# Busy TensorE products ahead of four norms and routings, and the last expert combine moved to TensorE, in a macaron block

## The chip, the cores and the metric

One core of one Trainium2 chip. The metric is the device time of one execution in microseconds (us); the time of a kernel is the median of its runs. Engines in the profile: PE is TensorE (PEld its weight loads), DVE is VectorE, ACT is ScalarE, POOL is GpSimd, SP is SyncE; SPq and POOLq are the queues from which SP and POOL start transfers. The clock granted to TensorE is printed as a share: 1.00 is 2.4 GHz, 0.50 is 1.2 GHz.

## The reference, cut to what matters

Four sequences of 256 tokens with 256 channels, all fp32. LN is a layer norm without gains.

```python
x += 0.5 * moe(LN(x))           # 64 experts, top 6 of a softmax, 64 slots each, plus a shared SiLU expert
x += attn16(LN(x))              # 16 heads, rotary, causal
x += 0.5 * moe(LN(x))           # the same weights again
x += 0.5 * wave(LN(x))
x += gqa(LN(x))                 # 16 query heads, 4 key heads
x += 0.5 * wave(LN(x))

def wave(x):
    h = (cos(ph) + sin(ph)) * sigmoid(x @ amp_w + amp_b)      # ph = pi * tanh(x @ ph_w + ph_b)
    for l in range(2):
        h = LN(h + (h @ ent_w[l] + ent_b[l]) @ ent_pw[l] + ent_pb[l])
        h = LN(h + sum over two paths of (h @ path_w[l, q] + path_b[l, q]) * mod[l, q])
    return h
```

In `moe` every token's row goes to the slots of its six experts, and its result is the sum of six expert rows, each times its weight. This sum of six rows is the *combine*.

## The kernel before, in words

The 1024 tokens are 8 tiles of 128, two for a sequence, and `m.x` holds them in SBUF for the whole program. PSUM is eight banks (`m.banks`). The program is a row of blocks; inside a block every engine has its own list of instructions in written order, and semaphores join the lists. Between two blocks all engines meet at a barrier.

**first_phase** routes the four sequences, one turn each. `norm_tensor` (L172) turns the normed tokens, `route_tensor` (L282) makes the router's logits (L238), half of the shared expert (L246), the rank of each token among those that chose the same expert (L255 to L258, it waits for DVE's choice mask), the other half, and the shared expert's output. DVE makes the slots (L383), and POOL sends the rows out with 12 indirect transfers (L434).

**experts_phase** runs the 64 experts over what SP loads from the slots (L700). **middle_phase** gathers and combines the first MoE, runs attention by sequence and routes again; three of the four routings run beside the attention of the next sequence, and the last stands alone after it, with `norm_tensor` and `route_tensor` in a row. `ahead(0, step)` is the first sequence's norm and projections (L172, L922). **experts_phase** then runs again.

`keep_busy(n)` (L931) issues n bf16 products of 128x384 into PSUM that nobody reads. The kernel before has it inside attention only.

**fold_phase** does two things at once. It folds the wave weights: `ent_w @ ent_pw` on PE (L1733, L1738), the path weights times `mod` on DVE, then bias, mean and last-row corrections. Beside that it combines the second MoE: POOL gathers 48 pieces of 128 rows (L1610), and DVE adds each to x with one multiply-add (L1634, and L1645 for the last sequence). Sequences share two buffers, so POOL waits for `s_combined`. When tiles 0 to 3 are done, POOL takes the root of their variance (L1968, L1970), DVE applies the norm (L1915), and PE and ACT begin the wave's first products (`wave_tensor_x`: turn L1801, product L1814; ACT takes tanh and a sine argument).

**last_phase** does the same for tiles 4 to 7, and meanwhile finishes the folded maps (`finish_maps`, L1539 to L1561, with `split_bias` L1521 to L1527 and `bias_for_last_row` L1534) and the attention weights (L1564 to L1571); POOL adds a bias to x over all tiles (L1985). Then ACT takes eight sines, DVE forms u (L1928), and 32 items (4 steps by 8 tiles) go through PE, ACT, DVE and a POOL root for each (L1968, L1970). Attention and the second wave follow.

## Time and profile before

| what | us |
|---|---|
| median of three runs (784.13, 786.36, 787.07) | 786.36 |
| profiled execution | 787.34 |
| span in its trace | 785.7 |
| PE busy | 577.7 (74%) |
| DVE busy | 389.2 (50%) |
| POOL busy | 295.2 (38%) |
| ACT busy | 233.4 (30%) |

The profiled execution lies 0.98 us above the median, and 1.6 us of it lie outside the span. Times inside the trace count from the start of the span. Busy times are sums over all stages; in one stage an engine can wait for the whole time while another sets the pace.

### The profile page before, as it was taken

To read this page: it belongs to the slowest core of one execution; us is meant where nothing else is said; L and a number is where in the kernel's file an instruction comes from. 1 tells how busy PE (TensorE), PEld (TensorE's weight loads), DVE (VectorE), ACT (ScalarE), POOL (GpSimd) and SP (SyncE) were. 2 spreads that over 40 slices of the span, in tenths; PEclk is the share of its full clock that TensorE was granted. 3 is DMA by queue.
4 is the path that set the end of the run, shared out by engine and by line. 5 is a ranking of instruction groups with operands and counts; after the bars stand their busy time and mean duration, and the time that the engine had idled before them with its cause. 6 is when DMAs were issued, how large, how long until landed. Compare 5 with 4: busy or idle time off the path is not lost. (4 is left out here: it accounts for less than half of the span.)

```text
span 785.7 us, 10359 instructions
## 1 busy us (share of the span) xinstructions
PE 577.7 (74%) x3486; PEld 368.9 (47%) x3486; DVE 389.2 (50%) x1102; ACT 233.4 (30%) x638; POOL 295.2 (38%) x383
## 2 busy tenths in 40 slices
PE   2666259970799999998953398984336697897796
PEld 1334125530466666665632254564213586554485
DVE  4656213333475676855442033366758547624135
ACT  1222024440132232321310144420033463142664
POOL 0556611106601537160326012257754266003065
PEclk9757569995799999998985599987577798998899
DMA  8886048842200314340166168733370000000001
GB/s 322 290 295 215 16 129 271 282 164 80 73 9 1 81 41 85 35 170 4 37 241 138 55 211 301 243 104 98 89 80 1 0 1 1 1 1 0 2 1 53
DMA packets 39723, 82.96 MB, mean 106 GB/s; under 512 B 7805, under 2 KB 27906, under 8 KB 38816
## 3 DMA queue, kind: packets, MB, share of 16 engines
q1 hardware_dynamic: 26144, 45.03, 17.7%
q0 software_dynamic: 13248, 37.07, 17.2%
q8 instruction: 25, 0.41, 0.2%
q10 hardware_dynamic: 288, 0.30, 0.1%
q14 instruction: 18, 0.15, 0.1%
HBM read 60.21 MB, written 26.35 MB: 110 GB/s over the span
## 5 line engine op out<-in xcount | busy, mean ns | idle before, releaser
L434 POOL DMA_INDIRECT expert_in<-xn_sent,scatter_slots x72 | 70.9, 985 | 79.7 <-DVE slots L383 50.5
L770 DVE SCALAR_TENSOR_TENSOR work<-work,banks 128x96 f32<-128x96 f32 x64 | 16.3, 254 | 124.1 <-ACT work L750 124.1
L1845 PE MATMUL banks<-w_gu,w_dn 128*128 128x256 f32 x256 | 68.4, 394 | 0.0
L1610 POOL DMA_INDIRECT w_dn<-expert_out,slots x48 | 51.3, 1069 | 26.4 <-issue 14.2
L790 PE MATMUL banks<-ident,work 128*128 128x128 f32 x128 | 29.5, 316 | 42.6 <-DMA work<-expert_in 42.6
L1251 POOL DMA_INDIRECT w_gu<-expert_out,gather_slots x48 | 49.3, 1028 | 28.7 <-DVE gather_slots L1259 14.7
L799 PE MATMUL banks<-w_gu,work 128*64 128x192 f32 x512 | 58.5, 352 | 0.0
L1968 POOL TENSOR_TENSOR var_eps<-mv,eps 128x1 f32<-128x1 f32 (+1 forms) x70 | 13.7, 195 | 116.8 <-ACT w_dn L1894 55.2
L1845 PEld LDWEIGHTS banks<-w_gu,w_dn 128*128 128x128 f32 x256 | 46.0, 199 | 4.2
L790 PEld LDWEIGHTS banks<-ident,work 128*128 128x128 f32 x128 | 13.8, 149 | 67.5 <-issue 41.5
L1970 POOL TENSOR_TENSOR rstd<-var_eps,minus_half 128x1 f32<-128x1 f32 (+1 forms) x70 | 42.4, 606 | 5.5
L1933 DVE TENSOR_SCALAR w_dn<-banks,rstd 128x255 f32<-128x255 f32 x48 | 23.2, 483 | 37.2 <-POOL rstd L1970 37.2
L812 PE MATMUL banks<-w_dn,work 96*64 96x256 f32 x256 | 41.4, 404 | 0.0
L746 ACT COPY work<-banks 128x256 f32<-128x256 f32 x64 | 23.8, 372 | 54.0 <-PE banks L790 54.0
L799 PEld LDWEIGHTS banks<-w_gu,work 128*64 128x64 f32 x512 | 32.6, 142 | 14.3 <-issue 11.2
L172 PE MATMUL banks<-ident,xn 128*128 128x128 f32 x24 | 5.3, 358 | 43.9 <-DVE xn L151 27.0
L1192 DVE TENSOR_REDUCE w_dn<-banks 128x2 f32<-128x256 f32 x64 | 31.6, 549 | 9.1 <-PE banks L978 8.7
L756 ACT COPY work<-banks 128x256 f32<-128x256 f32 x64 | 23.8, 372 | 36.0 <-PE banks L812 35.9
L1835 PE MATMUL banks<-ident,w_dn 128*128 128x128 f32 x128 | 25.7, 292 | 11.9 <-DVE w_dn L1928 11.9
L246 PE MATMUL banks<-w_sgu,work 128*128 128x384 f32 x64 | 34.1, 681 | 0.0
L1128 ACT ACTIVATE w_dn<-banks 128x768 f32<-128x768 f32 x32 | 26.0, 811 | 26.9 <-PE banks L1007 26.6
L163 POOL TENSOR_TENSOR rstd<-var_eps,minus_half 128x2 f32<-128x2 f32 x8 | 5.7, 713 | 74.9 <-DVE var_eps L142 48.8
(271 smaller groups left out, 1258.0 us busy)
## 6 DMA issues: line engine op xcount, KB each, us to landing
work<-expert_in SPq DMA_DIRECT2D x64, 128.0 KB, 3.8
expert_out<-work SPq DMA_DIRECT2D x64, 128.0 KB, 3.8
w_gu<-in_gate_up SPq DMA_DIRECT2D x10, 768.0 KB
w_gu<-in_gate_up POOLq DMA_DIRECT2D x6, 768.0 KB, 5.6
expert_in<-w_dn SPq DMA_DIRECT2D x4, 1024.0 KB, 7.5
w_dn<-in_down SPq DMA_DIRECT2D x10, 384.0 KB
w_gu<-in_gate_up SPq DMA_DIRECT2D x1, 3840.0 KB, 12.0
w_dn<-in_down SPq DMA_DIRECT2D x1, 3072.0 KB, 25.8
```

The lines of the kernel that those rows point to most:

```text
L246: last = nc.tensor.matmul(r.p_shared[t][:, 0:2 * SHID], r.xnT[:, c, t * P:(t + 1) * P], m.w_sgu[:, c, :], start=(c == 0), stop=(c == KC - 1))
L434: nc.gpsimd.indirect_dma_start(out=m.expert_in, out_offset=bass.IndirectOffsetOnAxis(m.scatter_slots[u][:, at:at + 1], 0), in_=xn[:, t, :] ...
L790: last = nc.tensor.transpose(p_rowsT[b % 2][:, c, :], rows[b][:, c * P:(c + 1) * P], m.ident[:, :])
L799: last = nc.tensor.matmul(p_gu[b % 2][half], rowsT[b % 2][:, c, half], w_gu[:, pair * 2 + e, c, :], start=(c == 0), stop=(c == KC - 1))
L812: last = nc.tensor.matmul(p_out[b % 2][half], hiddenT[b % 2][0:HID, half], w_dn[:, pair * 2 + e, :], start=True, stop=True)
L1128: nc.scalar.activation(a.pT[p % SLOTS3], a.p_pairs[p % SLOTS3], ACT.Exp).then_inc(s.probs, 1)
L1192: last = nc.vector.tensor_reduce(a.qk[:, tile, head + at:head + at + 2, DH], a.p_pairs[(p + 1) % SLOTS3][:, :, cols], AX.X, ALU.max, negat ...
L1251: nc.gpsimd.indirect_dma_start(out=rows[:, at, :], out_offset=None, in_=m.expert_out, in_offset=bass.IndirectOffsetOnAxis(m.gather_slots[: ...
L1610: nc.gpsimd.indirect_dma_start(out=w.combined[q % 2][:, t * TOPK + k, :], out_offset=None, in_=m.expert_out, in_offset=bass.IndirectOffset ...
L1835: last = nc.tensor.transpose(f.p_turn[t % DEEP][:, c, :], u[:, t, c * P:(c + 1) * P], m.ident[:, :])
L1845: last = nc.tensor.matmul(f.p_lin[t % DEEP], f.uT[t % DEEP][:, c, :], w.lin[:, step, c, :], start=(step > 0 and c == 0), stop=(c == KC - 1))
L1970: nc.gpsimd.tensor_tensor(m.rstd[:, group], m.var_eps[:, group], m.minus_half[:, group], ALU.pow).then_inc(done, 1)
```

## The change

Three edits.

1. `keep_busy` takes a bank. `route_tensor` issues 4 unread products ahead of the logits, 14 ahead of the rank and 4 ahead of the shared output, in the four turns of the first phase and in the last routing. In the middle phase PE waits until the first sequence's expert rows have been gathered and then issues 16 ahead of the first norm, and 14 ahead of the last routing's norm.
2. The fold moves into the last phase: one block less. `finish_maps` becomes `scale_maps` and `finish_qkv`, called from the fold's DVE list.
3. The second combine moves to PE. ACT writes each weight column as a 128x128 diagonal (a ring of 8), PE multiplies it with the gathered rows, six products a tile added up in PSUM (`sum_tile`), and DVE adds the sum to x (`add_sum`). The rows have seven homes, and the last tile takes the first home again, so POOL's last six gathers wait for tile 0's sum. The norm goes by tiles 0 to 3, 4 and 5, 6 and 7. All eight sines come behind the last product.

```diff
 def route_tensor(nc, m, r, eng, s, ready, turn, then=None):
+    keep_busy(nc, m, 4, FREE_BANK)
     route_tensor_logits(nc, m, r, eng, s, ready)
     route_tensor_shared(nc, m, r, s, 0)
+    keep_busy(nc, m, 14, FREE_BANK)
     route_tensor_rank(nc, m, r, eng, s, turn)
...
+    keep_busy(nc, m, 4, FREE_BANK)
     route_tensor_out(nc, m, r, eng, s, turn)
...
-def keep_busy(nc, m, n):
+def keep_busy(nc, m, n, bank=2):
...
+            pe.wait_ge(comb.gathered[TB - 1], 16 * TOPK)
+            keep_busy(nc, m, 16)
             for step in range(3):
                 ahead(0, step)
...
+            keep_busy(nc, m, 14)
             norm_tensor(nc, m, pe, norm, 2 * B - 1, m.xn_sent, p_norm)
             route_tensor(nc, m, r, pe, sr, (norm.xnT, 2 * B), 2 * B - 1)
...
+def fold_pool(nc, m, w, s, wave, pool):
+    for t in range(TILES):
+        if t == 7:
+            pool.wait_ge(s.summed, 1)
+        for k in range(TOPK):
+            nc.gpsimd.indirect_dma_start(
...
+        if t == 5:
+            norm_roots_pool(nc, m, wave, pool, 0, [0])
+        if t == 6:
+            norm_roots_pool(nc, m, wave, pool, 0, [1])
+    norm_roots_pool(nc, m, wave, pool, 0, [2])
...
+def fold_vector(nc, m, w, f, s, wave, dve, chain):
...
+    for k in range(1, STEPS):
+        nc.vector.tensor_copy(w.shift_wide[:, k - 1], w.shift_cols[:, k - 1, :].unsqueeze(2).broadcast_to([P, KC, P])
+                              ).then_inc(s.wide, 1)
+    add_sum(0)
+    add_sum(1)
...
+    scale_maps(nc, w, dve, chain, s.scaled)
+    for t in range(2, 4):
+        add_sum(t)
+    stats_all_vector(nc, m, wave, chain, range(0, 4))
+    add_sum(4)
+    split_bias(nc, m, w, chain)
+    apply_all_vector(nc, m, f, wave, dve, 0, range(0, 4))
+    for k in range(1, STEPS):
+        dve.wait_ge(s.last_steps, k)
+        bias_for_last_row(nc, m, chain, w.lin[:, k], m.banks[:, 4 + k, 0:D], w.bias[:, 2 + k, :])
+    dve.sem_inc(s.maps, 1)
+    add_sum(5)
+    stats_all_vector(nc, m, wave, chain, range(4, 6))
+    dve.wait_ge(s.small, 4 * 16)
+    finish_qkv(nc, w, chain)
+    add_sum(6)
+    stats_all_vector(nc, m, wave, chain, range(6, 7))
+    apply_all_vector(nc, m, f, wave, dve, 0, range(4, 6))
+    add_sum(7)
+    stats_all_vector(nc, m, wave, chain, range(7, 8))
+    apply_all_vector(nc, m, f, wave, dve, 0, range(6, 8))
...
+    sum_tile(0)
+    sum_tile(1)
+    for k in range(1, STEPS):
+        step_shift(k)
+    sum_tile(2)
+    sum_tile(3)
+    pe.wait_ge(s.scaled, 1)
...
+    sum_tile(4)
+    pe.wait_ge(s.maps, 1)
+    wave_tensor_x(nc, m, w, f, wave, pe, 0, range(0, 4), f.p_turn_x)
+    sum_tile(5)
+    sum_tile(6)
+    wave_tensor_x(nc, m, w, f, wave, pe, 0, range(4, 6), f.p_turn_x)
+    sum_tile(7)
+    wave_tensor_x(nc, m, w, f, wave, pe, 0, range(6, 8), f.p_turn_x)
```

TensorE in one routing turn of the first phase, before: the logits, half of the shared expert, the rank and the other half.

```order
L238 MATMUL banks<-w_router,work 128x64 [waits norm_normed_T_ready]
L238 MATMUL banks<-w_router,work 128x64 x3
L246 MATMUL banks<-w_sgu,work 128x384 x2
L255 MATMUL banks<-work,before_b 128x64 [waits route_choice_mask_ready]
L256 MATMUL banks<-taken,ones_b 128x64
```

The same place in the changed kernel, whose line numbers are its own; L937 is `keep_busy`.

```order
L937 MATMUL banks<-causal_b,ident_b 128x384 x4
L241 MATMUL banks<-w_router,work 128x64 [waits norm_normed_T_ready]
L241 MATMUL banks<-w_router,work 128x64 x3
L249 MATMUL banks<-w_sgu,work 128x384 x2
L937 MATMUL banks<-causal_b,ident_b 128x384 x14
L258 MATMUL banks<-work,before_b 128x64 [waits route_choice_mask_ready]
```

The busy products stand ahead of each wait, so the logits and the rank are queued behind them.

GpSimd in the fold, before: gathers, the first norm's root, the last gathers, the barrier and the second root.

```order
L1610 DMA w_dn<-expert_out,slots 128x256 x24
L1610 DMA w_dn<-expert_out,slots 128x256 [waits sequence_combined]
L1610 DMA w_dn<-expert_out,slots 128x256 x11
L1968 TENSOR_TENSOR var_eps<-mv,eps 128x4 [waits wave_x_variance_ready,sequence_combined]
L1970 TENSOR_TENSOR rstd<-var_eps,minus_half 128x4 [waits wave_eps_added]
L1610 DMA w_dn<-expert_out,slots 128x256 x12
```

GpSimd at the same place in the changed kernel: L1613 is a gather, L2034 and L2036 are a norm's root.

```order
L1613 DMA w_dn<-expert_out,slots 128x256 x24
L1613 DMA work<-expert_out,slots 128x256 x12
L2034 TENSOR_TENSOR var_eps<-mv,eps 128x4 [waits wave_x_variance_ready]
L2036 TENSOR_TENSOR rstd<-var_eps,minus_half 128x4 [waits wave_eps_added]
L1613 DMA w_qkv<-expert_out,slots 128x256 x6
L2034 TENSOR_TENSOR var_eps<-mv,eps 128x2 [waits wave_x_variance_ready]
L2036 TENSOR_TENSOR rstd<-var_eps,minus_half 128x2 [waits wave_eps_added]
L1613 DMA w_dn<-expert_out,slots 128x256 [waits tile_summed]
L1613 DMA w_dn<-expert_out,slots 128x256 x5
```

The last six gathers (tile 7) now stand behind the root of tiles 4 and 5, which waits for DVE's statistics of these tiles.

TensorE in the changed kernel, from the sum of tile 4 (L1763) to the sum of tile 6; L1866 turns, L1879 multiplies.

```order
L1763 MATMUL banks<-work,w_dn 128x256 [waits weight_diagonal_ready,last_rows_gathered_tile4,tile_sum_added]
L1763 MATMUL banks<-work,w_dn 128x256 [waits weight_diagonal_ready] x5
L1866 MATMUL banks<-ident,w_dn 128x128 [waits wave_x_normed,step_maps_ready]
...
L1879 MATMUL banks<-w_gu,w_dn 128x512 [waits wave_x_T_ready]
L1879 MATMUL banks<-w_gu,w_dn 128x512
L1763 MATMUL banks<-work,w_dn 128x256 [waits weight_diagonal_ready,last_rows_gathered_tile5,tile_sum_added]
L1763 MATMUL banks<-work,w_dn 128x256 [waits weight_diagonal_ready] x5
L1763 MATMUL banks<-w_qkv,w_dn 128x256 [waits weight_diagonal_ready,last_rows_gathered_tile6,tile_sum_added]
```

The first wave products of tiles 0 to 3 now wait for the finished maps (`step_maps_ready`), and the sums of tiles 5 to 7 come behind them.

## Rows read from the trace of the kernel before

**Rows 1.** The page's part 4: the chain that ended last, by engine.

```profile
issue 9%; POOL 6%; PE 5%; DVE 3%; POOLq 0%; ACT 0%; DVEq 0%
```

**Rows 2.** Timeline, PE, first routing turn: start, length, line, operation, idle before and releaser.

```profile
16.01 1.97 PE L238 MATMUL banks<-w_router,work 128*128 128x64 f32 x8 [0.67 <-ACT work L179]
...
22.16 0.20 PE L255 MATMUL banks<-work,before_b 128*128 128x64 bf16 x1 [1.84 <-DVE work L349]
```

**Rows 3.** Timeline, second turn: DVE's slots, and POOL's first scatter.

```profile
42.52 0.17 DVE L383 COPY slots<-scatter_slots 128x12 uint32<-128x12 uint32 x1
...
48.83 0.97 POOL L434 DMA_INDIRECT expert_in<-xn_sent,scatter_slots  x1 [6.91 <-remote]
```

**Rows 4.** Timeline, PE, a stretch of the second attention at the full clock.

```profile
242.18 2.82 PE L922 MATMUL banks<-w_qkv,w_gu 128*128 128x512 f32 x8
...
252.00 3.41 PE L931 MATMUL banks<-causal_b,ident_b 128*128 128x384 bf16 x20
...
256.53 1.10 PE L238 MATMUL banks<-w_router,work 128*128 128x64 f32 x8 [0.68 <-ACT work L179]
```

**Rows 5.** Timeline, DVE and PE, ahead of the first attention.

```profile
194.03 3.09 DVE L1275 SCALAR_TENSOR_TENSOR x<-w_gu,cur_weights,x 128x256 f32<-128x256 f32 x6 [4.87 <-DMA w_gu<-expert_out,gather_slots]
...
199.88 1.08 PE L172 MATMUL banks<-ident,xn 128*128 128x128 f32 x4 [27.04 <-DVE xn L151]
201.63 8.37 PE L922 MATMUL banks<-w_qkv,w_gu 128*128 128x512 f32 x16 [0.67 <-ACT w_gu L179]
```

**Rows 6.** Timeline, PE and SP's queue, the last routing and the load behind it.

```profile
404.75 0.76 PE L172 MATMUL banks<-ident,xn_sent 128*128 128x128 f32 x4 [3.56 <-DVE xn_sent L151]
406.18 1.97 PE L238 MATMUL banks<-w_router,work 128*128 128x64 f32 x8 [0.68 <-ACT work L179]
...
441.61 8.53 SPq L700 DMA_DIRECT2D work<-expert_in  x8
```

**Rows 7.** Timeline, PE, fold and first wave.

```profile
515.86 9.99 PE L1733 MATMUL banks<-w_gu 128*128 128x256 f32 x32 [2.69 <-PEq L694]
...
594.66 1.54 PE L1801 MATMUL banks<-ident,w_dn 128*128 128x128 f32 x6 [17.70 <-DVE w_dn L1915]
596.00 3.62 PE L1814 MATMUL banks<-w_gu,w_dn 128*128 128x512 f32 x4
...
599.84 5.46 PE L1814 MATMUL banks<-w_gu,w_dn 128*128 128x512 f32 x12
```

**Rows 8.** Timeline, POOL, DVE and ACT, fold and first wave.

```profile
566.61 1.04 POOL L1970 TENSOR_TENSOR rstd<-var_eps,minus_half 128x4 f32<-128x4 f32 x1
...
582.48 1.00 POOL L1610 DMA_INDIRECT w_dn<-expert_out,slots  x1 [0.30 <-issue]
...
588.68 3.09 DVE L1645 SCALAR_TENSOR_TENSOR x<-w_dn,weights,x 128x256 f32<-128x256 f32 x6 [5.67 <-DMA w_dn<-expert_out,slots]
...
606.75 1.28 ACT L1885 ACT_TABLE_LOAD   x1
...
615.20 2.77 DVE L1928 SCALAR_TENSOR_TENSOR w_dn<-w_dn 128x256 f32<-128x256 f32 x8
```

**Rows 9.** Four stretches: length; PE, PEld, DVE, ACT, POOL busy; clock, DMA share, GB/s.

```profile
524.73:532.27 7.54, 7.54 (x37) 6.65 (x36) 7.06 (x14) 0.00 (x0) 6.02 (x6) 1.00 0.35 102
563.26:565.30 2.04, 2.04 (x6) 1.59 (x6) 1.97 (x2) 0.00 (x0) 1.43 (x3) 0.50 0.39 96
595.49:598.93 3.44, 3.44 (x8) 1.73 (x7) 3.41 (x4) 1.02 (x3) 3.28 (x1) 0.50 0.00 0
602.46:612.84 10.38, 4.40 (x13) 2.01 (x11) 9.81 (x25) 7.41 (x16) 0.13 (x1) 0.88 0.01 2
```

**Rows 10.** DVE's groups by line in the fold: busy, mean ns, idle before.

```profile
L1545 DVE TENSOR_SCALAR w_gu<-w_gu 128x4 f32<-128x4 f32 x1 | 3.5, 3476 | 0.0
...
L1903 DVE BATCH_NORM_STATS2 stats<-x 128x6 f32<-128x256 f32 x8 | 3.0, 418 | 0.4
...
L1717 DVE TENSOR_TENSOR w_gu<-w_gu,banks 128x256 f32<-128x256 f32 x3 | 1.3, 420 | 1.2 <-PE banks L1746 1.1
```

More of the change, by code:

```diff
@@ L1477, in last_weights @@
     w.parts = [g[:, first:first + 128].bitcast(BF16) for first in (8192, 8960, 3072)]
-    w.combined = [flat(d, 10240 + 3072 * b, (TB * TOPK, D)) for b in range(2)]
+    one = TOPK * D
+    homes = [d[:, 10240 + one * b:10240 + one * (b + 1)] for b in range(4)]
+    homes += [m.work[:, 0:one], m.work[:, one:2 * one], m.w_qkv[:, :, :].rearrange("p c n -> p (c n)"), homes[0]]
+    w.combined = [home.rearrange("p (k d) -> p k d", d=D) for home in homes]
     return w
@@ L1556, in finish_maps, with finish_qkv @@
     eng.sem_inc(s_scaled, 1)
-    split_bias(nc, m, w, chain)
-    for k in range(1, STEPS):
-        eng.wait_ge(s_last, k)
-        bias_for_last_row(nc, m, chain, w.lin[:, k], m.banks[:, 4 + k, 0:D], w.bias[:, 2 + k, :])
-    eng.sem_inc(s_ready, 1)
+def finish_qkv(nc, w, chain):
     for c in range(KC):
@@ new lines, with __init__ @@
+class Fold:
+    def __init__(self, sem):
+        self.small = sem("small_last_weights_loaded")
+        self.prod, self.read = sem("fold_product_ready"), sem("fold_products_read")
+        self.wide = sem("bias_columns_spread")
+        self.halved, self.last = sem("amplitude_map_halved"), sem("last_row_of_input_maps_ready")
+        self.sin, self.half = sem("phase_sines_ready"), sem("phase_reduced")
+        self.gathered = [sem(f"last_rows_gathered_tile{t}") for t in range(TILES)]
+        self.diag, self.used = sem("weight_diagonal_ready"), sem("weight_diagonal_used")
+        self.summed, self.added = sem("tile_summed"), sem("tile_sum_added")
+        self.maps, self.scaled, self.last_steps = sem("step_maps_ready"), sem("step_maps_scaled"), sem("last_row_of_step_maps_ready")
@@ new lines, in fold_scalar, with diagonals @@
+def fold_scalar(nc, m, w, f, s, wave, act):
+    def diagonals(t):
+        for k in range(TOPK):
+            j = t * TOPK + k
+            if j >= DIAGS:
+                last_used = j - DIAGS
+                if last_used % TOPK == TOPK - 1:
+                    act.wait_ge(s.summed, last_used // TOPK + 1)
+                else:
+                    act.wait_ge(s.used, last_used - last_used // TOPK + 1)
+            nc.scalar.activation(w.diag[j % DIAGS], m.ident[:, :], ACT.Copy, scale=m.weights[:, t, k:k + 1]
+                                 ).then_inc(s.diag, 1)
+    act.wait_ge(s.half, 1)
+    nc.scalar.activation(w.phase_sin, w.phase_turns, ACT.Sin).then_inc(s.sin, 1)
+    act.wait_ge(s.half, 2)
+    nc.scalar.activation(w.phase_cos, w.phase_cos, ACT.Sin, scale=-1.0, bias=w.half_pi).then_inc(s.sin, 1)
+    for t in range(6):
+        diagonals(t)
+    wave_scalar_x(nc, w, f, wave, act, 0, range(0, 4))
+    diagonals(6)
+    diagonals(7)
+    wave_scalar_x(nc, w, f, wave, act, 0, range(4, 6))
+    wave_scalar_x(nc, w, f, wave, act, 0, range(6, 8))
@@ L2027, in _ @@
         def _(dve):
[L2028 removed]
             chain = Chain(dve, v_chain)
[L2030 to L2031 removed]
+            fold_vector(nc, m, w, f, fold, wave, dve, chain)
+            wave_vector(nc, m, w, f, wave, dve, chain, 0)
             dve.wait_ge(s_pad, 3)
@@ L2044, in _ @@
         def _(pe):
-            def last_rows():
-                pe.wait_ge(s_scaled, 1)
-                pe.wait_ge(wave.tanh, TILES)
-                for k in range(1, STEPS):
-                    nc.tensor.matmul(m.banks[:, 4 + k, 0:D], w.last_row, w.lin[:, k, KC - 1, :], start=True, stop=True
-                                     ).then_inc(s_last, 1)
-            wave_tensor(nc, m, w, f, wave, pe, 0, s_maps, REST, last_rows)
+            fold_tensor(nc, m, w, f, fold, wave, pe)
+            wave_tensor(nc, m, w, f, wave, pe, 0, fold.maps)
             for t in range(TILES):
```

360 lines of the change are left out of this document (164 added, 196 removed).

## The prediction

> **What bounds the kernel now.** I read the chain that ended last first. No engine holds it: the largest share is issue, and POOL, PE and DVE have a few per cent each [rows 1]. So time is won or lost in the waits of single stages, and I went through the timelines of the four stages that the change touches.
>
> In the first routing, PE waits 0.67 us for the turned norm and 1.84 us for DVE's choice mask [rows 2]. From the second turn on the route is not what POOL waits for: DVE has the slots at 42.7, and POOL's first scatter starts at 48.83, released by the completion of the turn before it [rows 3]. Six microseconds of slack lie between them. Only a delay of the first turn reaches the end.
>
> Ahead of the first attention PE has been idle for 27.04 us, and then it works at the lower clock: the 16 projection passes take 8.37 us [rows 5], where 8 of the same take 2.82 us in a stretch at the full clock [rows 4]. Ahead of the last routing PE is idle for 3.56 us, and its logits take 1.97 us [rows 6] against 1.10 us at the full clock [rows 4].
>
> The fold is the long case. The first wave can't go on before DVE forms u at 615.20 [rows 8]. Three chains end near there: POOL's gathers (the last is issued at 582.48, and DVE has its rows at 588.68, 5.2 us after the issue ended); PE's cold products of tiles 4 to 7, from 594.66 to 605.3 [rows 7]; and DVE's finish of the maps, which ends last. DVE's list runs without a hole into u; the sines that ACT makes behind its table load of 1.28 us are there before. So the change has to beat u's start at 615.20.
>
> **The change part by part.**
>
> *First routing.* A busy product is 3.41 / 20 = 0.17 us at the full clock [rows 4]; the logits double at the lower one, so I take 0.30 to 0.34 us there. The 4 ahead of the logits need up to 1.3 us where the hole is 0.67: the logits start some 0.6 us late. The 14 ahead of the rank need 2.4 us at the full clock or 4.5 us at the lower one, in a hole of 1.84 us [rows 2], less what the faster logits give back. If the clock has risen by then the turn loses about 1.0 us in all; if not, 2.9; if everything after it runs faster, 0. PE has been working off and on from 14 us, so I take +1.0. In turns two to four the six microseconds of slack cover even the worst of these [rows 3]; without that cover each would cost the same again.
>
> *First attention.* The new wait ends when the last rows are gathered, which is DVE's start at 194.03; 16 products at 0.17 to 0.34 us end between 197 and 199.4, ahead of the turn at 199.88 [rows 5]. PE then has 5 us of work behind it. In the first wave PE began cold at 594.66, and its products from 599.84 on already run at the full price [rows 7]; the projections would begin as late behind the first busy product. The turn (1.08) falls by 0.4 us and the projections from 8.37 to 5.6, together −3.3 us. The least is −1.5 (the clock rises in their middle), the most −3.6. Nothing waits behind these products: PE had nothing else to do. Beside them DVE and POOL go on as before.
>
> *Last routing.* 14 products fit the 3.56 us hole at the full clock, which PE has from attention, and 4 fit 0.68 us. The logits fall by 0.87 us [rows 4, 6], the rank and the slots come about 1.1 us sooner, and with them POOL's scatters. How much of it reaches SP's first load of expert rows at 441.61 is open, since the weights of the experts are loaded again at the same time. Between −1.2 and, if the products run cold and block the rank, +1; I take half of the gain, −0.6.
>
> *The fold.* I follow the new lists from 515.86, where PE starts in both kernels.
> PE folds both layers, two stretches like the first of 9.99 us [rows 7], the second with a full clock shorter, and makes the last row of the amplitude map: 533.5. DVE then has a bias correction of 2.0 us, mod and one layer's path maps and copies (7.5 us), and the second layer without mod (6.2) [rows 9]: the shift columns are spread at 549.7. In before these stood between the combines, so DVE's time per piece is the same, but PE now waits for them from the second sum on and has cooled.
> Six shift products cold, twice the full price of 0.45 us each [rows 7], take 5.1 us: 554.8, and DVE adds until 555.2. From there DVE's chain is: the reductions (3.4 us) and their scaling, the rest of the map's work (10.4 us) [rows 9], three sums to add (3 x 0.42), four tiles of statistics (4 x 0.42 and the aggregates), four tiles of norm (1.6) [rows 10], together 19.4 us; with 0.8 us of waiting for PE the maps are ready at 575.4. In before one of these steps was stretched: 128x4 values took 3476 ns under POOL's bias add [rows 10]. That is gone, and I count 0.3 us for both such steps. The Trainium skill, SBUF — State Buffer, section "SBUF: two separate sides", calls the port pair that DVE and GpSimd share an exclusive lock that is held for a whole instruction; the row agrees.
> PE now does the wave products of tiles 0 to 3. They are the same as those of tiles 4 to 7 in before, 10.6 us with the cold start [rows 7]: 586.0. The sum of tile 5 is 12 passes of half of 5.46 / 12 each, 2.7 us at the full clock and 5.4 at the lower one; with its add, its statistics and those of tile 4, tiles 4 and 5 are ready at 590.4. POOL's root (0.3 and 1.04 us [rows 8]) ends at 591.7. Only now POOL may issue tile 7's gathers: six at 1.3 us end at 599.5. The rows landed 5.2 us behind the last of twelve in before [rows 8]; between 0 and that I take half, 2.7, since six gathers alone queue less: 602.2. PE has little to do then, so tile 7's sum takes 2.7 to 5.4 us; I take 4.6: 606.8. Add, statistics, root and norm take 3.2: 610.0. Turn, copy and products of tiles 6 and 7, partly cold, take 5.4; tanh, the argument, the table load (1.28) and the first sine take 3.1. **u starts at 618.5**, 3.3 us later than now. DVE's 48 multiply-adds are gone, but DVE is not what ends last any more, so this gives nothing by itself. The dropped barrier, POOL's bias add and its memsets lie under the sines and the first u.
> Its bounds: 608 with the full clock throughout (−7), 625.5 with the lower clock throughout and the latest landing (+10.3).
>
> The sum: +1.0 − 3.3 − 0.6 + 3.3 = +0.4 us. The profiled execution is 0.98 us above the median of the runs; a difference holds for either, so I set it on the median: 786.36 + 0.4 = **786.8 us**. About 0.5% (3.9 us) is what a measurement of this kernel can tell from no change: 782.4 and 790.3 are the borders.
>
> **The rivals.**
> (a) *POOL's hold doesn't matter.* If tiles 4 and 5 have their statistics early, tile 7's gathers follow tile 6's at once, u starts near 605 and the sum is 0.4 − 13.5, some 773 to 777 us. For it: POOL has nothing else to do. Against it: their sums stand behind the wave products of tiles 0 to 3 in PE's list, and these behind the maps. Chance 0.09.
> (b) *PE is cold through the fold's end*, the side on which it gets slower. The sum of tile 7, the turns and the products of tiles 6 and 7 come after holes of 3 us and more, and the fold's first stretches after 10. If each runs at the lower clock and the rows land 5.2 us late, u starts at 624 to 625.5 and the sum is +6 to +7.4: 793 us. It decides from u at 622 on. For it: in before PE came to these very products cold after 17.70 us idle, at 3.62 us for 4 passes against 5.46 for 12 [rows 7]. Against it: its waits now are shorter. Chance 0.2.
> (c) *The busy products delay what they should help.* Cold in the first turn and in the last routing, they add 2.9 and 1.0 instead of 1.0 and −0.6: 790.3. Chance 0.06.
> (d) *The busy products do not raise the clock.* The first attention stays at 8.37 us and the last routing at 1.97: +3.3 and +0.6, 790.7 us. In before the products at 599.84 had the full clock after a cold start [rows 7]. The Trainium skill, TensorE: Matmul & The Clock Gate, section "What's actually happening", says that the moment of the change varies from run to run, and asks not to count on a certain number of slow products. By that rule the sum would lose most of its −3.3. One trace can't show it. Chance 0.05.
>
> **How the numbers follow.** The forecast, within 3.9 us of the old time, has 0.60. Faster comes from (a) and from 0.08 of the forecast's 0.60, where PE stays warm through the fold: 0.17. Slower comes from (b) and half of (c) and (d): 0.26. Same is the rest, 0.57. The range leaves out (a) and the far half of (b): 780.5 to 792.5.
>
> **What would show it.** In the changed trace the projections of the first attention should take about 5.6 us, at a clock of 1.00. POOL should stand idle from about 574 to 590 in the fold, released by the statistics of tiles 4 and 5, with six gathers behind it; u should start at 618.5 and DVE should wait for ACT's first sine there. If DVE's last map work ends behind the sines, or if POOL's last gathers come before 585, the fold's sum is wrong. If the first slots of turn one come over 2 us later, the first term is. What would overturn the forecast most is the fold: a clock that stays up gives 7 us more than I count, and a cold one takes 7.

## The result

The changed kernel takes **791.31 us** (median of 6 runs), the kernel before 786.64 us (6 runs): ratio **1.0057**, 95% interval 1.0032 to 1.0082, which is 2.5 to 6.5 us slower. One of its six runs, 803.86 us, was a slow run; the ratio leaves it out, and the median of the other five is 790.64. The forecast was 786.8, no change, with a range of 780.5 to 792.5. The time lies in the range, near its upper end; the value was 4.5 us too low, and the loss is a little over the 0.5% (3.9 us) that I had set as the border of "same", with an interval on both sides of it. By that border the change is slower, which had a chance of 0.26, and not the same, which had 0.57. One of the two effects was about right and the other was priced at under half of what it costs.

The profiled execution of the changed kernel took 789.74 us (a span of 788.0) and lies 1.6 us under the median of its runs, so its trace shows only part of the loss: 2.3 us of span. It was gained and lost like this, each stage from its own start, so that what came ahead of it does not count:

| stage | before | after | difference |
|---|---|---|---|
| start to PE's first fold product | 515.86 | 508.65 | −7.2 |
| fold product to the first u | 99.3 | 104.3 | +5.0 |
| first u to the fifth root of the wave | 10.1 | 12.5 | +2.4 |
| fifth root to the end | 160.4 | 162.5 | +2.1 |

The fold's first product, to be laid beside the first line of [rows 7]:

```profile
508.65 15.74 PE L1778 MATMUL banks<-w_gu 128*128 128x256 f32 x64 [2.69 <-PEq L700]
```

The first row holds more than the products' work. The expert rows for the first attention have been gathered at 192.24, ahead of the 16 products, where it was 194.03; and from the last routing's first load of expert rows to the fold it takes 73.3 us where it took 74.3. No edit was to gain these 2.7 us. Of the last row 1.4 us are one group of PE's transposes in the attention between the two waves, 3.36 us in place of 1.96, and no edit touches it.

The chain that ended last now names PE and DVE where POOL stood behind issue [rows 1].

```profile
PE 11%; issue 8%; DVE 8%; POOL 6%; POOLq 0%; ACT 0%; DVEq 0%
```

**The products ahead of the routings and the first attention.** Timeline of PE, first routing turn, to be laid beside [rows 2]; L172 is the norm's turn, L937 `keep_busy`, L241 the logits, L258 the rank. The first line is the norm's turn before, the others are the changed kernel's.

```profile
14.25 1.09 PE L172 MATMUL banks<-ident,xn 128*128 128x128 f32 x4 [14.25 <-DVE xn L564]
```

```profile
13.79 1.09 PE L172 MATMUL banks<-ident,xn 128*128 128x128 f32 x4 [13.79 <-DVE xn L570]
14.67 1.49 PE L937 MATMUL banks<-causal_b,ident_b 128*128 128x384 bf16 x4
15.95 1.81 PE L241 MATMUL banks<-w_router,work 128*128 128x64 f32 x8
...
19.07 2.44 PE L937 MATMUL banks<-causal_b,ident_b 128*128 128x384 bf16 x14
21.96 0.20 PE L258 MATMUL banks<-work,before_b 128*128 128x64 bf16 x1 [0.44 <-DVE work L355]
```

By their length the first four run at the lower clock (0.37 us each), but the 14 ahead of the rank already at the full one (0.17); the profile's column of the granted clock reads 1.00 in both stretches, so here only the lengths tell. In this trace the rank still waits 0.44 us for DVE after them. Counted from the norm's turn it starts 8.17 us later (21.96 − 13.79), where it was 7.91 (22.16 − 14.25): the turn loses 0.26 us, which the times as they stand hide, because the norm came 0.46 us sooner in this trace.

PE ahead of the first attention, against [rows 5]: 16 products begin when the rows are gathered, PE still waits 1.41 us for the norm, and the projections take 5.43 us.

```profile
192.24 4.30 PE L937 MATMUL banks<-causal_b,ident_b 128*128 128x384 bf16 x16 [21.21 <-DMA w_gu<-expert_out,gather_slots]
197.95 0.76 PE L172 MATMUL banks<-ident,xn 128*128 128x128 f32 x4 [1.41 <-DVE xn L151]
199.39 5.43 PE L928 MATMUL banks<-w_qkv,w_gu 128*128 128x512 f32 x16 [0.67 <-ACT w_gu L179]
```

The last routing, PE and SP's queue, against [rows 6].

```profile
399.49 0.76 PE L172 MATMUL banks<-ident,xn_sent 128*128 128x128 f32 x4 [1.29 <-DVE xn_sent L151]
...
400.92 1.10 PE L241 MATMUL banks<-w_router,work 128*128 128x64 f32 x8
...
435.35 8.28 SPq L706 DMA_DIRECT2D work<-expert_in  x8
```

From the norm's turn to the first load of expert rows it is 35.86 us, where it was 36.86 (441.61 − 404.75): the whole microsecond arrives.

**The fold.** Timeline of PE against [rows 7]: the wave products of tiles 0 to 3 (L1866, L1879), the sums of tiles 5 and 7 (L1763), and the products of tiles 6 and 7.

```profile
568.19 1.84 PE L1866 MATMUL banks<-ident,w_dn 128*128 128x128 f32 x6 [8.64 <-DVEq L1736]
...
573.66 5.63 PE L1879 MATMUL banks<-w_gu,w_dn 128*128 128x512 f32 x12
579.13 2.75 PE L1763 MATMUL banks<-work,w_dn 128*128 128x256 f32 x12
...
596.66 2.83 PE L1763 MATMUL banks<-w_dn 128*128 128x256 f32 x12 [3.09 <-issue]
602.49 1.09 PE L1866 MATMUL banks<-ident,w_dn 128*128 128x128 f32 x4 [2.99 <-DVE w_dn L1983]
603.61 6.07 PE L1879 MATMUL banks<-w_gu,w_dn 128*128 128x512 f32 x8
```

PE stands idle for 8.64 us ahead of the maps, with the sum of tile 5 queued behind the products that wait for them. The last eight passes take 6.07 us; at the full clock they take 3.70 (below). The granted clock in 602.49 to 608:

```profile
602.49:608.00 5.51, 5.47 (x9) 2.50 (x10) 0.17 (x1) 1.32 (x3) 5.26 (x2) 0.50 0.00 0
```

POOL, against [rows 8]: after tile 6's last gather it waits 14.99 us for the statistics of tiles 4 and 5, and only then issues tile 7's gathers.

```profile
567.62 1.00 POOL L1613 DMA_INDIRECT w_qkv<-expert_out,slots  x1 [0.30 <-issue]
583.61 0.19 POOL L2034 TENSOR_TENSOR var_eps<-mv,eps 128x2 f32<-128x2 f32 x1 [14.99 <-DVE mv L1973]
...
591.52 0.99 POOL L1613 DMA_INDIRECT w_dn<-expert_out,slots  x1 [0.31 <-issue]
```

DVE: the two short steps that were stretched before [rows 10] take 0.17 us each, DVE waits 13.84 us for the sum of tile 5, and forms u at 612.96, released by ACT's sines.

```profile
551.06 0.17 DVE L1558 TENSOR_SCALAR w_gu<-w_gu 128x4 f32<-128x4 f32 x1
...
581.92 0.42 DVE L1655 TENSOR_TENSOR x<-x,banks 128x256 f32<-128x256 f32 x1 [13.84 <-PE banks L1763]
...
612.96 3.22 DVE L1994 SCALAR_TENSOR_TENSOR w_dn<-w_dn 128x256 f32<-128x256 f32 x8 [10.30 <-ACT w_dn L1952]
```

ACT around the first u: eight sines in a row, and then the copies (L1957) of the turned u, on which PE's first products wait.

```profile
612.41 3.30 ACT L1952 ACTIVATE w_dn<-w_dn,w_gu 128x256 f32<-128x256 f32 x8
615.62 0.88 ACT L1957 COPY w_dn<-banks 128x256 f32<-128x256 f32 x3
```

The first roots on POOL. Before, the first came 4.60 us after u (619.80 − 615.20), now 5.76. Before, the second followed 1.94 us later and the rest 1.19 us apart; now the next two follow 2.35 and 2.04 us apart.

```profile
618.72 0.19 POOL L2034 TENSOR_TENSOR var_eps<-mv,eps 128x1 f32<-128x1 f32 x1 [9.06 <-ACT w_dn L1961]
...
621.07 0.19 POOL L2034 TENSOR_TENSOR var_eps<-mv,eps 128x1 f32<-128x1 f32 x1 [1.52 <-ACT w_dn L1961]
...
623.11 0.19 POOL L2034 TENSOR_TENSOR var_eps<-mv,eps 128x1 f32<-128x1 f32 x1 [1.21 <-ACT w_dn L1961]
```

### The profile page after: what moved, and what is told of

Same layout as the page of the kernel before. It is cut to its first block and busy times, and to the rows that moved or that the text cites. A ratio compares the mean times of both kernels' runs of the same rounds, so it can differ in the third digit from the quotient of the medians.

```text
span 788.0 us, 10859 instructions
## 1 busy us (share of the span) xinstructions
PE 615.4 (78%) x3722; PEld 396.4 (50%) x3722; DVE 369.1 (47%) x1062; ACT 249.6 (32%) x686; POOL 295.1 (37%) x385
## 3 DMA queue, kind: packets, MB, share of 16 engines
q0 software_dynamic: 13248, 37.07, 17.1%
## 5 line engine op out<-in xcount | busy, mean ns | idle before, releaser
L937 PE MATMUL banks<-causal_b,ident_b 128*128 128x384 bf16 x254 | 52.4, 357 | 25.7 <-DMA w_gu<-expert_out,gather_slots 21.2
L2034 POOL TENSOR_TENSOR var_eps<-mv,eps 128x1 f32<-128x1 f32 (+2 forms) x71 | 13.7, 193 | 125.7 <-DVE mv L1973 74.9
L937 PEld LDWEIGHTS banks<-causal_b,ident_b 128*128 128x128 bf16 x254 | 26.6, 106 | 46.6 <-issue 28.2
L2036 POOL TENSOR_TENSOR rstd<-var_eps,minus_half 128x1 f32<-128x1 f32 (+2 forms) x71 | 42.5, 599 | 5.6
L1613 POOL DMA_INDIRECT w_dn<-expert_out,slots x30 | 33.1, 1104 | 20.9 <-POOLq L700 12.2
L1879 PE MATMUL banks<-w_gu,w_dn 128*128 128x512 f32 x64 | 36.8, 723 | 0.0
L762 ACT COPY work<-banks 128x256 f32<-128x256 f32 x64 | 23.8, 372 | 36.0 <-PE banks L818 35.9
L1961 ACT ACTIVATE w_dn<-banks 128x256 f32<-128x256 f32 x64 | 24.5, 383 | 29.5 <-PE banks L1911 29.5
## 6 DMA issues: line engine op xcount, KB each, us to landing
w_gu<-in_gate_up SPq DMA_DIRECT2D x1, 3840.0 KB, 11.8
```

The lines of the kernel that those rows point to most:

```text
L937: nc.tensor.matmul(m.banks[:, bank, 0:3 * P], m.ident_b[:, 0:P], m.causal_b[:, :], start=True, stop=True)
L1613: nc.gpsimd.indirect_dma_start(out=w.combined[t][:, k, :], out_offset=None, in_=m.expert_out, in_offset=bass.IndirectOffsetOnAxis(m.slots[ ...
L1879: last = nc.tensor.matmul(f.p_z[t % DEEP], f.uT[t % DEEP][:, c, :], w.amp_ph[:, c, :], start=(c == 0), stop=(c == KC - 1))
L2034: nc.gpsimd.tensor_tensor(m.var_eps[:, group], src, m.eps[:, group], ALU.add).then_inc(s.eps, 1)
L2036: nc.gpsimd.tensor_tensor(m.rstd[:, group], m.var_eps[:, group], m.minus_half[:, group], ALU.pow).then_inc(done, 1)
```

## The experiments

The theory after the result: the products win 2 to 5 us and the fold loses more than twice the 3.3 us I gave it, through the order of PE's list (sum 5 behind the maps), through POOL's hold, and through the lower clock at the end of the fold. Its rivals: that the products lose by delaying the rank, that the clock is chance and the products are worth nothing, and that the combine on PE is dear in itself, whatever the order. Every ratio is to runs of the kernel before that were taken beside the experiment (medians of 785.77 to 786.75 us).

### The two halves apart

**e1** is the kernel before with the first edit alone; **e2** is the changed kernel without it.

```diff
 # e2, against the changed kernel
-    keep_busy(nc, m, 4, FREE_BANK)
     route_tensor_logits(nc, m, r, eng, s, ready)
     route_tensor_shared(nc, m, r, s, 0)
-    keep_busy(nc, m, 14, FREE_BANK)
     route_tensor_rank(nc, m, r, eng, s, turn)
...
-    keep_busy(nc, m, 4, FREE_BANK)
     route_tensor_out(nc, m, r, eng, s, turn)
...
-            pe.wait_ge(comb.gathered[TB - 1], 16 * TOPK)
-            keep_busy(nc, m, 16)
...
-            keep_busy(nc, m, 14)
             norm_tensor(nc, m, pe, norm, 2 * B - 1, m.xn_sent, p_norm)
```

Expected of e1:

> The kernel before with the first edit alone (all unread products, no change of the fold). Theory A, the forecast's own terms: +1.0 in the first turn, -3.3 ahead of the first attention, -0.6 in the last routing, so 2.9 us faster (ratio 0.996). Theory B, read from the changed trace: the first turn loses only some 0.3 us, the first attention gains 3.3 and the last routing 1.0, so 4 to 5 us faster (0.994 to 0.995). Rival C, the moment of the clock varies so much from run to run that the products are worth nothing on the whole: ratio 0.999 to 1.001. In the trace the last routing should reach its logits at the full price of 1.10 us, and DVE's u should start 4 to 6 us ahead of 615.20 with the fold as long as before.

Expected of e2:

> The changed kernel without any of the added unread products, so that only the fold and the second combine differ from the kernel before. Theory A, the forecast's term: u starts 3.3 us later and nothing else moves, ratio 1.004. Theory B, read from the changed trace: u is 3.9 us late, counted from PE's first fold product, and PE comes to the first items of the wave cold, which costs 2.4 us more, and up to 1.5 later on, so 6 to 8 us slower (1.008 to 1.010). Rival C, the fold costs nothing in itself and the 4.7 us are those products that delay the rank: ratio 1.000 +- 0.002.

e1: 784.22 us (12 runs), ratio 0.9970 (0.9945 to 0.9994). e2: 794.65 us (6 runs), ratio 1.0111 (1.0075 to 1.0147). The products win 2.4 us (0.5 to 4.3), the fold costs 8.7 us (5.9 to 11.6). The rivals that the products lose or are worth nothing, and that the fold is free, fall; for the products it is narrow, since 1.000 lies just outside the interval. The two halves add up to +6.3 us where the whole change cost 4.5, which the intervals allow. Theory A was right for e1 (−2.9) and wrong for e2 (+3.3): the term of the fold is what failed. In e1's trace u starts at 611.73, 3.5 us ahead of 615.20 where 4 to 6 were expected, and the fold is as long as before (99.3). In e2's trace the fold takes 104.6 us to the first u, as in the changed kernel. Its sum of tile 7 begins a little sooner, 86.6 us behind the first fold product (512.87) where it was 88.0, but waits longer and runs cold. Without any of the products this fold still starts 3.0 us sooner than in before.

```profile
599.49 4.47 PE L1757 MATMUL banks<-w_dn 128*128 128x256 f32 x12 [4.59 <-issue]
```

### The products apart

**e3** has only the 16 products ahead of the first attention, **e10** only those of the routings and the 14 ahead of the last norm (both on the kernel before).

```diff
 # e3, against the kernel before
+            pe.wait_ge(comb.gathered[TB - 1], 16 * TOPK)
+            keep_busy(nc, m, 16)
             for step in range(3):
                 ahead(0, step)
```

Expected of e3:

> The kernel before with the 16 unread products ahead of the first attention alone. If the clock answers to them as forecast, the projections take 5.4 to 5.7 us in place of 8.37 and the kernel gains 3.3 us (ratio 0.9958). If the gain of the first edit lies mostly in the last routing, it is under 1.5 us (over 0.998).

Expected of e10:

> The kernel before with the unread products of the routings alone (4, 14 and 4 in each stand-alone routing and 14 ahead of the last norm), without the 16 ahead of the first attention. The forecast's terms: +1.0 in the first turn and -0.6 in the last routing, +0.4 us in all (ratio 1.0005). By the traces so far the first turn loses nothing and the last routing wins 1.0 us, all of which arrives at the load of the expert rows: 1.0 us faster (0.9987). Neither can be told from no change by the time alone; the trace should show 35.9 us from the last routing's norm to the first load where it was 36.9.

e3: 784.29 us, ratio 0.9971 (0.9948 to 0.9993). e10: 783.76 us, ratio 0.9965 (0.9939 to 0.9991). e3 fell between its two expectations and e10 beyond its own: e3 wins 2.3 us where 3.3 were expected, e10 wins 2.8 (0.7 to 4.8) where 1.0 was. The times of e3 and e10 do not add up to e1's 2.4, and with intervals of 4 us they cannot tell the halves apart. The traces can. In e3 the projections fall to 5.43 us:

```profile
201.46 5.43 PE L922 MATMUL banks<-w_qkv,w_gu 128*128 128x512 f32 x16 [0.67 <-ACT w_gu L179]
```

and in e10 they stay at the old price while the last routing's logits are at the full clock:

```profile
201.05 8.05 PE L928 MATMUL banks<-w_qkv,w_gu 128*128 128x512 f32 x16 [0.68 <-ACT w_gu L179]
...
404.12 1.10 PE L241 MATMUL banks<-w_router,work 128*128 128x64 f32 x8
```

From the last norm's turn (402.68) to the first load of expert rows (438.56) it is 35.9 us in e10, as expected. What the other 1.8 us of e10 are, if they are any, stays open.

### POOL's hold

**e4** puts tile 7's gathers ahead of the root of tiles 4 and 5.

```diff
-        if t == 6:
-            norm_roots_pool(nc, m, wave, pool, 0, [1])
-    norm_roots_pool(nc, m, wave, pool, 0, [2])
+    norm_roots_pool(nc, m, wave, pool, 0, [1, 2])
```

> The changed kernel with POOL's last six gathers ahead of the root of tiles 4 and 5, so that they are not held by it. By the forecast's rival (a) u starts 10 us or more earlier and the kernel is 10 to 13 us faster than the changed one (ratio to before about 0.990 to 0.993). By the changed trace TensorE ends the products of tiles 4 and 5 at 593.6 and begins the sum of tile 7 at 596.66, so that the hold costs 3.1 us and some of the clock behind it: 3 to 6 us faster than the changed kernel (ratio to before 0.998 to 1.002). If the hold is hidden behind TensorE anyway: no difference to the changed kernel (1.005 to 1.006).

784.97 us (12 runs), ratio to before 0.9965 (0.9933 to 0.9998); with the changed kernel at 1.0057 that is 7.2 us less (about 4 to 10 by the two intervals), more than the 3 to 6 that the changed trace gave. The hold was real and lay on the path: the third expectation falls. Rival (a)'s price of 10 to 13 us lies at the edge of what the intervals allow, or beyond. TensorE now goes from the products of tiles 4 and 5 into the sum of tile 7 with no wait:

```profile
593.88 5.33 PE L1877 MATMUL banks<-w_gu,w_dn 128*128 128x512 f32 x8
599.06 2.75 PE L1761 MATMUL banks<-w_dn 128*128 128x256 f32 x12
```

But this one trace does not show 7 us. Its run took 788.84 us, near the top of twelve that lie between 780.3 and 792.1, four of them under 781; its first attention ran partly cold (7.12 us), and the products of tiles 4 and 5 were no warmer than in the changed kernel (5.33 us, 5.12 there). Its fold takes 102.6 us to u, 1.7 less than in the changed kernel. Even this is no more than chance can do: e7's fold is the changed kernel's up to u, and takes 102.3. How the 7.2 us divide is not shown.

### The order of PE's list

**e8** moves one sum, and leaves POOL's list as the change made it.

```diff
     sum_tile(4)
+    sum_tile(5)
     pe.wait_ge(s.maps, 1)
     wave_tensor_x(nc, m, w, f, wave, pe, 0, range(0, 4), f.p_turn_x)
-    sum_tile(5)
     sum_tile(6)
```

> The changed kernel with the sum of tile 5 on TensorE moved ahead of its wait for the maps, into the 8.6 us in which it stood idle; POOL's lists are untouched, so the root of tiles 4 and 5 still stands ahead of the last six gathers. If those gathers were late because that root waited for a sum queued behind the wave products of tiles 0 to 3, the statistics come right after the maps, POOL goes on about 14 us sooner, and the kernel is as fast as with the gathers ahead of the root, or up to 2.7 us faster: ratio to before 0.993 to 0.997. If the late gathers had another cause (the wait for tile 0's sum, the transfers themselves), only the 2.7 us of the sum are won: 1.002.

782.19 us (12 runs), ratio 0.9948 (0.9925 to 0.9971), by the two ratios 8.6 us under the changed kernel, in the first expectation's range; the 2.7 us of the sum alone do not explain it. POOL's wait for the statistics shrinks from 14.99 to 3.45 us, and the sum runs in what was the hole:

```profile
574.58 0.19 POOL L2034 TENSOR_TENSOR var_eps<-mv,eps 128x2 f32<-128x2 f32 x1 [3.45 <-DVE mv L1973]
```

```profile
564.02 2.83 PE L1763 MATMUL banks<-work,w_dn 128*128 128x256 f32 x12 [0.21 <-issue]
...
584.45 2.83 PE L1763 MATMUL banks<-w_qkv,w_dn 128*128 128x256 f32 x12 [1.86 <-ACT w_dn L1635]
```

So the gathers were late because of a root that waited for a sum that stood behind products that waited for the maps. Its one trace, of a run of 784.82 us near the top of the twelve, shows 4.2 us of the gain up to u (100.1 in place of 104.3) and 1.6 from u to the fifth root. The last line above shows what is late next: the sum of tile 6 waits for ACT's diagonals, which ACT's list has behind the wave's activations.

**e5** takes both (POOL's list as in e4, the sum of tile 5 as in e8), and puts the sums of tiles 6 and 7 together ahead of the products of tiles 4 and 5; ACT makes tile 6's diagonals before the wave.

```diff
     sum_tile(4)
+    sum_tile(5)
     pe.wait_ge(s.maps, 1)
     wave_tensor_x(nc, m, w, f, wave, pe, 0, range(0, 4), f.p_turn_x)
-    sum_tile(5)
     sum_tile(6)
+    sum_tile(7)
     wave_tensor_x(nc, m, w, f, wave, pe, 0, range(4, 6), f.p_turn_x)
-    sum_tile(7)
     wave_tensor_x(nc, m, w, f, wave, pe, 0, range(6, 8), f.p_turn_x)
...
-    for t in range(6):
+    for t in range(7):
         diagonals(t)
     wave_scalar_x(nc, w, f, wave, act, 0, range(0, 4))
-    diagonals(6)
     diagonals(7)
```

> The changed kernel with the gathers of tile 7 ahead of the root of tiles 4 and 5, the sum of tile 5 ahead of the wait for the maps, and the sums of tiles 6 and 7 ahead of the products of tiles 4 and 5, so that TensorE has no hole between the maps and the last product. Counted from the changed trace: products of tiles 0 to 3 until 579, two sums until 585, products of tiles 4 to 7 at the full clock until 594, the first u near 597 in place of 613: 12 to 16 us faster than the changed kernel, ratio to before 0.985 to 0.991. If the cold clock and not the order makes the stage long, 6 to 8 us as with the gathers alone (0.996).

774.45 us (5 runs), ratio **0.9845** (0.9820 to 0.9870): 12.2 us under the kernel before (785.77 × 0.0155), by the two ratios 16.7 under the changed one, a little more than the first expectation. The sum of the same parts in another order: the rival that the combine on PE is dear in itself falls. How the 8 us by which e5 lies under e8 divide among its three moves is not shown. PE from the sums to the last product, without a wait over 1.3 us and at the full clock, and DVE's first u:

```profile
580.95 2.75 PE L1760 MATMUL banks<-w_qkv,w_dn 128*128 128x256 f32 x12
583.54 2.75 PE L1760 MATMUL banks<-w_dn 128*128 128x256 f32 x12
586.13 0.60 PE L1863 MATMUL banks<-ident,w_dn 128*128 128x128 f32 x4
586.98 3.70 PE L1876 MATMUL banks<-w_gu,w_dn 128*128 128x512 f32 x8 [0.24 <-ACT w_dn L1924]
590.52 0.60 PE L1863 MATMUL banks<-ident,w_dn 128*128 128x128 f32 x4
592.42 3.70 PE L1876 MATMUL banks<-w_gu,w_dn 128*128 128x512 f32 x8 [1.30 <-ACT w_dn L1924]
```

```profile
599.40 3.22 DVE L1991 SCALAR_TENSOR_TENSOR w_dn<-w_dn 128x256 f32<-128x256 f32 x8 [9.96 <-ACT w_dn L1949]
```

From the first fold product (508.98) it is 90.4 us to u; before it was 99.3, in the changed kernel 104.3.

### The cold start of the items

**e7** is the changed kernel with 12 products ahead of the first u; **e6** is e5 with those and with 8 and 12 more in the fold's own holes; **e9** is e5 with 22 ahead of u, up to its start, and 5 behind the third turn.

```diff
 # e9, against e5
+    keep_busy(nc, m, 22, 3)
     eng.wait_ge(s_maps, 1)
     for n in range(ITEMS + LAG):
         if n < ITEMS:
             turn_u(n, n // TILES, n % TILES)
+        if n == LAG:
+            keep_busy(nc, m, 5, 3)
```

Expected of e7:

> The changed kernel with 12 unread products on TensorE ahead of the first u of both waves, nothing else. The changed trace has the first roots of the first wave 2.35 and 2.04 us apart where later ones are 1.19 and then 1.08 apart. If that is TensorE's lower clock, the first wave wins 2.0 and the second 1.2 us: ratio to before 1.001 to 1.003 in place of 1.006. If the start is slow because of ACT's copies or u itself, nothing changes (1.005 to 1.007).

Expected of e6:

> The same with unread products in three more holes of TensorE: 8 ahead of the wait for the scaled maps, 12 ahead of the wait for the finished maps, and 12 ahead of the first u of both waves. If TensorE's lower clock is what the stage still pays for, the products of tiles 0 to 3 fall from 10.6 to about 8 us and the first items of each wave lose their 1.2 to 2.4 us: 4 to 6 us faster than without them. If the clock's moment is chance, no difference (+-1 us), and if the products fill more than their holes, slower.

Expected of e9:

> The kernel with the sums ahead (e5), and 22 unread products ahead of the first u of both waves, which fill its 3.85 us hole to the end, and 5 more between the third turn and the first product, where TensorE waits 1.1 us for ACT. If the slow start of a wave's items is the lower clock, which falls in these two holes, the first roots come 1.2 us apart from the start, and the kernel is 2 to 4 us faster than without the products (ratio to before 0.980 to 0.983); 12 products alone left a hole behind them and the clock fell in it. If the slow start has another cause, nothing changes: 0.984 to 0.986.

e7: 789.59 us, ratio 1.0047 (1.0020 to 1.0074), between its two expectations and not to be told from the changed kernel. e6: 771.89 us, 0.9839 (0.9810 to 0.9868), where 4 to 6 us under e5 were expected (0.977 to 0.979). e9: 773.51 us, **0.9834** (0.9809 to 0.9860). Against e5's 0.9845 neither e6 nor e9 can be told apart by time; e9 just missed the 0.980 to 0.983 that was expected. In e6's trace the products of tiles 0 to 3 did fall to 8.4 us (572.10 to 580.54), but u came no sooner (90.7 us behind the first fold product, 90.4 in e5), since the sum of tile 7 then waited 2.58 us and ran cold. The traces say why e7 gave little: its products end 1.9 us ahead of the first turn, behind the turns PE waits 1.34 us for ACT, and the granted clock falls there. Three stretches of e7 from the first of these products on; the granted clock is the number behind POOL's busy time:

```profile
608.82:612.83 4.01, 2.12 (x13) 1.10 (x12) 0.57 (x2) 3.78 (x7) 1.05 (x3) 1.00 0.00 0
612.83:616.83 4.00, 2.66 (x11) 1.80 (x12) 2.65 (x7) 2.98 (x9) 0.00 (x0) 0.62 0.00 0
616.83:620.83 4.00, 4.00 (x14) 3.13 (x13) 0.48 (x1) 1.60 (x6) 1.13 (x4) 0.52 0.00 0
```

In e9 both holes are nearly full (0.27 and 0.54 us are left), and the clock stays at 1.00 throughout:

```profile
595.00:605.00 10.00, 9.18 (x53) 5.86 (x52) 3.63 (x9) 8.14 (x21) 1.75 (x6) 1.00 0.00 0
```

The first two roots are 1.19 us apart from the start:

```profile
603.72 0.19 POOL L2034 TENSOR_TENSOR var_eps<-mv,eps 128x1 f32<-128x1 f32 x1 [7.76 <-ACT w_dn L1961]
604.91 0.19 POOL L2034 TENSOR_TENSOR var_eps<-mv,eps 128x1 f32<-128x1 f32 x1 [0.36 <-ACT w_dn L1961]
```

From u to the fifth root it is 9.6 us, against 11.8 in e5, 12.5 in the changed kernel and 10.9 to 12.2 in the other traces with the new fold. The second wave says the same in all twelve traces. The first pair of roots is before's, the second e9's:

```profile
745.11 0.19 POOL L1968 TENSOR_TENSOR var_eps<-mv,eps 128x1 f32<-128x1 f32 x1 [20.09 <-ACT w_dn L1894]
...
747.46 0.19 POOL L1968 TENSOR_TENSOR var_eps<-mv,eps 128x1 f32<-128x1 f32 x1 [1.52 <-ACT w_dn L1894]
```

```profile
730.17 0.19 POOL L2034 TENSOR_TENSOR var_eps<-mv,eps 128x1 f32<-128x1 f32 x1 [19.24 <-ACT w_dn L1961]
...
731.36 0.19 POOL L2034 TENSOR_TENSOR var_eps<-mv,eps 128x1 f32<-128x1 f32 x1 [0.37 <-ACT w_dn L1961]
```

In ten traces, before among them, the first root of the second wave comes 5.76 or 5.77 us behind its u and the next 2.30 to 2.35 later; in e9 and e6 it is 4.81 and 1.19. e7 and e6 have the same 12 products there, and only e6 gains by them: how many are enough is not shown. That the slow start is the clock is shown by these stretches; that it is worth 2 us of the total time is not, since the runs scatter by as much. e5, e6 and e9 are the fastest kernels of all, and cannot be told from each other.

## Why the prediction was right or wrong

The sum of the first three terms, −2.9, agrees with e1's −2.4, but in part by luck, since their errors go both ways: the first was too dear, the second too large and the third too small.

**The first routing, +1.0:** too dear for what arrives, though the turn does pay. Counted from the norm's turn, DVE's slots come 10.9 to 11.0 us later in the three traces without these products, and 10.8 to 11.4 us in seven of the nine with them. In the other two, e6 and e8, it is 12.7 and 12.9 us: the 14 products ran partly cold there, and the rank started right behind them without a wait for DVE. This is e8's row, against the 2.44 us above:

```profile
20.70 3.69 PE L937 MATMUL banks<-causal_b,ident_b 128*128 128x384 bf16 x14
```

So the forecast's cases of 0, 1.0 and 2.9 us span what the turn lost, and a trace falls into one or the other. But less than half of it arrives: from the norm's turn to the first load of expert rows it is 90.4 to 90.8 us without the products, 89.1 to 90.7 in the seven, and 90.9 and 91.4 in e6 and e8. "Only a delay of the first turn reaches the end" was too strong.

**The first attention, −3.3:** the mechanism held. The projections fell to 5.43 us (5.6 forecast) in eight of nine traces that had the 16 products, and stayed at 7.12 in the ninth, e4's. The price was a little high: from the first norm's turn to the last routing's, 203.4 to 205.3 us in the three traces without them became 201.5 to 203.4 in the eight, and 204.9 in e4. On average 2.3 us are left, and e3's runs say 2.3. So about a third of the 3.3 us is given back before the last routing; where is not shown. The Trainium skill, TensorE: Matmul & The Clock Gate, section "What's actually happening", has the moment of the clock's change vary from run to run. The ninth trace agrees; that the gain goes with it, as rival (d) had it, does not follow from the other eight.

**The last routing, −0.6:** the gain was 1.0, in every trace with these products. I had halved it for doubt about the transfers beside it; 36.86 us from the norm to the first load became 35.86 to 35.88 (36.87 and 37.07 in e3 and e2, which lack them), so the transfers beside it take nothing of the gain.

**The fold, +3.3:** the term that failed, though most of its steps came out. Moved by the 7.21 us that the fold starts sooner, I had the maps at 568.2, and PE went on at 568.19; POOL's root of tiles 4 and 5 ending at 584.5, and it ended at 584.6; the last gather at 592.3, and it ended at 592.5. Then two misses cancelled, which is luck: the sum of tile 7 began 1.7 us late (the rows landed 4.2 us behind the issue, not 2.7) but ran at the full clock (2.83 us, not 4.6), so that the norm of tiles 6 and 7 was on time, at 602.65 for 602.8. What failed comes behind that. The turn, copy and products of tiles 6 and 7 took 7.2 us where I had 5.4, since the clock was at 0.50 from 602.49 to 608.00; that put u at 612.96 and not at 611.3. And my comparison ended at u: the sum had no term for what follows, where I had looked only for the barrier, POOL's bias add and its memsets. In before, the sines ended 3.9 us ahead of u (611.34); now they end at 615.71, behind its start, and ACT's copies of the first turned u stand behind them in its list. So the first root comes 5.76 us behind u and not 4.60, in seven of the eight traces with the new fold. With the clock this cost 2.4 us up to the fifth root in the changed trace; this goes with the trace, and in e2, e4 and e8 it is 0.8 us. Together it is +7.4 in the changed trace and +6.1 in e2's where I had +3.3; e2's runs say +8.7, with an interval that reaches down to 5.9. The largest thing in this stage is neither of the two: it is the order of PE's list, which I priced as it stood (below).

**The rivals.** (b), a cold end of the fold, is what happened, in part: the last turn and products were cold and the sum of tile 7 was not. u came 5.0 us late by the fold's own clock, between the forecast's 3.3 and the rival's 8.8 to 10.3, and short of the 6.8 (u at 622) from which the rival was to decide. I had named the place and given it 0.2. The range held because its upper end took in the near half of (b). (a) did not happen, and e4 puts its price lower, at 7.2 us and not 10 to 13, since PE was busy until 593.6 in any case. (c) and (d) as they were priced fall with e1, e3 and e10; in single traces both show in part, (c) in the first turn of e6 and e8, (d) in the first attention of e4.

**What I did not look at.** I followed PE's new list as given and priced its waits, and did not ask which of its pieces could have run in them. The 8.64 us hole ahead of the maps lay under the 19.4 us that I gave to DVE, and the sum of tile 5, whose rows came in time for it, stood behind the wave products that follow it. That one position cost 8.6 us (e8), nearly twice the whole loss of the change.

The two steps that POOL's bias add had stretched took 0.17 us each away from it, as forecast. In before it was not the bias add alone: that ended at 600.17, two memsets of POOL followed, and the longer step ended at 602.41, with the second of them (602.38). The Trainium skill, SBUF — State Buffer, section "SBUF: two separate sides", calls the shared port pair a lock; the trace agrees, with 3476 ns before, in that the step ended only with POOL's work.

## What to carry to other kernels

When work moves to an in-order engine, write its new list down with the time at which each piece's inputs are there, and look at every wait for a later piece that is already ready: here the same pieces in another order were 16.7 us apart. Follow a change past the point where the old bound stood, to the first stretch that repeats at its old pace, because what was hidden under the old bound (eight sines, the clock's rise) is now in the open. Products that nobody reads can keep the clock through a hole, but look in several traces how much of the hole they may leave: ahead of the first u, 12 of them with 1.90 and 1.34 us left over lost the clock and 22 and 5 up to the next work kept it, while ahead of the first attention 16 with 0.8 to 1.6 us left over did their work in eight of nine traces. And put them ahead of a wait only where they cannot outlast it: cold, 14 of them held the rank.

## What the runs showed of the hardware that was not expected

The granted clock can fall across a short wait. In e7 it was 1.00 in the 4.01 us up to 612.83, in which PE worked for 2.12 us, and on average 0.62 in the next 4.00 us, in which PE worked for 2.66. Stages that no edit touches differ by more than I had allowed: from the first load of expert rows after the last routing to the first fold product it took between 71.0 and 74.6 us in the twelve traces, the kernel before having 74.3, and from the fifth root to the end between 159.0 and 163.1. Two traces of one and the same fold, the changed kernel's and e7's, are 2.0 us apart up to u; its first 64 products alone took 15.74 us in the one and 14.05 in the other. With 1.6 us between the changed kernel's profiled run and its median, a single pair of traces can place a loss of 5 us, but not measure it.
